# A fused attention and mixture-of-experts kernel on one core: the last attention batch interleaved with the first weights batch, and a reordered passage to the experts

## The reference, cut to what matters

```python
def attn(x, w_qkv, w_out, b_out, norm_g, norm_b):          # x: (8, 512, 256), 16 heads of 16
    q, k, v = split_heads(einsum('bnm,om->bno', x, w_qkv))
    dots = einsum('bhid,bhjd->bhij', q, k)
    norm = sqrt(sum(dots * dots, axis=-1, keepdims=True))
    attn = dots / maximum(norm, 1e-12) * norm_g + norm_b
    return einsum('bnm,om->bno', merge(einsum('bhij,bhjd->bhid', attn, v)), w_out) + b_out

def ffn(x, norm_gamma, slot_norm_gamma, slot_embeds, w1, b1, w2, b2):
    xn, sn = rmsnorm(x, norm_gamma), rmsnorm(slot_embeds, slot_norm_gamma)
    logits = einsum('bnd,esd->bnes', xn, sn)               # 8 experts, 128 slots each
    dispatch = softmax(logits, axis=1)                     # over the tokens
    combine = softmax(logits.reshape(b, n, e * s), axis=-1)
    slots = einsum('bnd,bnes->besd', xn, dispatch)
    h = gelu(einsum('besd,edh->besh', slots, w1) + b1)     # hidden 1024
    eo = einsum('besh,ehd->besd', h, w2) + b2
    return einsum('bmd,bnm->bnd', eo.reshape(b, e * s, 256), combine)

x = x + layernorm(attn(layernorm(x), ...))
x = x + layernorm(ffn(layernorm(x), ...))
```

## Time and profile before

| | |
|---|---|
| median of 3 runs | 873.18 us (872.75 to 873.45) |
| profiled execution | 873.14 us |
| its span in the profile | 870.5 us |
| mean granted clock of TensorE | 0.989 |
| attention, to the last back | 0 to 159 us |
| the last back and weights batch 0 | 159 to 203 us |
| weights batches 1 to 7 | 203 to 396 us |
| passage to the experts | 396 to 416 us |
| experts | 416 to 773 us |
| combine | 773 to 870 us |

### The profile page before, as it was taken

The page is one execution under the profiler, slowest core; times in us unless marked ns, Lnnn a source line. Parts: engine busy times, 40 slices in busy tenths (PEclk is TensorE's granted clock), DMA queues, the critical chain, the costliest instruction groups (busy, mean ns, idle before and its releaser), DMA issues. The chain is left out here.

```text
span 870.5 us, 16018 instructions
## 1 busy us (share of the span) xinstructions
PE 841.5 (97%) x5368; PEld 752.0 (86%) x5368; DVE 619.1 (71%) x1192; ACT 538.7 (62%) x1061; POOL 94.2 (11%) x105
## 2 busy tenths in 40 slices
PE   6999999779999999997999999999999999999998
PEld 6998999667788888885899999999999999999997
DVE  7788887658999898998665556555656564267786
ACT  5556555458776667776655555554556464467775
POOL 1200000022373323433000000000000000000000
PEclk9999999889999999998999999999999999999999
DMA  7111121041222222222302020202020205026983
GB/s 219 38 49 49 48 72 49 25 139 68 87 97 97 96 96 96 93 78 102 117 23 75 3 95 1 96 0 96 0 96 0 96 0 194 1 62 227 286 269 123
DMA packets 52283, 75.32 MB, mean 87 GB/s; under 512 B 3088, under 2 KB 33424, under 8 KB 52112
## 3 DMA queue, kind: packets, MB, share of 16 engines
q1 hardware_dynamic: 52240, 74.76, 25.4%
HBM read 49.59 MB, written 25.17 MB: 86 GB/s over the span
## 5 line engine op out<-in xcount | busy, mean ns | idle before, releaser
L883 PEld LDWEIGHTS bank<-w_r,act_r 128*128 128x128 f32 x1536 | 200.8, 191 | 11.0 <-DVE act_r L1765 0.7
L883 PE MATMUL bank<-w_r,act_r 128*128 128x256 f32 x1536 | 204.0, 283 | 0.2 <-DVE act_r L1765 0.2
L866 PE MATMUL bank<-sl_r,w_r 128*128 128x512 f32 x768 | 200.6, 397 | 3.6 <-DVE sl_r L1745 3.6
L1765 DVE TENSOR_TENSOR act_r<-act,act_r 128x512 fp32r<-128x512 f32 x128 | 88.6, 692 | 151.0 <-ACT act_r L1263 151.0
L1258 ACT ACTIVATE act<-bank,b_sb 128x512 f32<-128x512 f32 x128 | 88.0, 687 | 153.0 <-PE bank L866 153.0
L866 PEld LDWEIGHTS bank<-sl_r,w_r 128*128 128x128 f32 x768 | 138.0, 192 | 27.1 <-issue 3.9
L791 PE MATMUL bank<-disp_r,y_r 128*128 128x512 f32 x384 | 103.4, 406 | 1.0 <-DVE disp_r L1678 0.9
L766 PE MATMUL bank<-yT_r,snT 128*128 128x512 f32 x384 | 100.1, 397 | 0.0
L919 PE MATMUL bank<-eo_r,comb_r 128*128 128x258 f32 x768 | 92.5, 282 | 0.5 <-DVE eo_r L386 0.5
L919 PEld LDWEIGHTS bank<-eo_r,comb_r 128*128 128x128 f32 x768 | 92.2, 189 | 0.7 <-issue 0.7
L766 PEld LDWEIGHTS bank<-yT_r,snT 128*128 128x128 f32 x384 | 72.6, 190 | 15.7
(11 more groups left out here) (170 smaller groups left out, 1152.1 us busy)
## 6 DMA issues: line engine op xcount, KB each, us to landing
stage<-in_w SPq DMA_DIRECT2D x16, 1024.0 KB, 6.8
combine_scratch<-comb SPq DMA_DIRECT2D x64, 256.0 KB, 2.0
stage<-combine_scratch SPq DMA_DIRECT2D x4, 2048.0 KB, 9.3
snT<-combine_scratch SPq DMA_DIRECT2D x4, 2048.0 KB, 10.1
x_scratch<-stage SPq DMA_DIRECT2D x8, 512.0 KB, 3.0
x<-x_scratch SPq DMA_DIRECT2D x8, 512.0 KB, 4.0
x_d<-x_scratch SPq DMA_DIRECT2D x8, 512.0 KB, 9.7
slots_eo<-in_x SPq DMA_DIRECT2D x7, 512.0 KB, 4.3
```

The costliest lines, as they stand in the source:

```text
L866: last = pe.matmul(bank[i % RING][:, :], w1_r[q][:, a, k, j * P:(j + 1) * P], sl_r[f][:, c, k, :], start=(n == 0), stop=(n == len(steps) - 1))
L883: last = pe.matmul(bank[4 + 2 * f + c // 2][:, (c % 2) * D:(c % 2 + 1) * D], act_r[:, i % RING, a, c * S:(c + 1) * S], w2_r[q][:, w, j, :] ...
L1765: v.tensor_tensor(act_r[:, i % RING, 1, :], act[:, i % 2, :], act_r[:, i % RING, 0, :].bitcast(F32), ALU.subtract).then_inc(h_split, 1)
```

## The change

The memory of the attention stage is laid out anew, so that batch 0 of the weights stage has tiles of its own (`neg_lt0` and `disp0` in unused halves of `slots_eo`, `neg_max0`, `z_disp0`, `rz_disp0`), and `run_min` is shared by both stages. The split slots of the experts, `sl_r`, lie in `snT`.

PE's, ACT's and DVE's last attention back and first weights batch become one list each, `last_back_and_first_weights`. y of batch 0 is made in `attention(B - 1, before_y=True)`. The roots of x2 (`root_x2`, `scale_y`) are taken for batches 0 to 3, 4 to 6 and 7 apart. The end of batch 7's attention (`square_proj`, `root_proj`, `add_proj`, `square_x2`) is cut into slices in weights batches 2, 3 and 4, its last root comes in batch 5; the sums and the centring of w2's rows are placed in batches 5 to 7. SP stores x2 of batch 7 and loads the first weights after batch 3's reloads. The loops of ACT and DVE over the weights batches are written out.

In the passage, ACT's and DVE's steps have a new order, both halves of w2's subtraction go from POOL to DVE, the second slots' split goes into the first expert, whose `expert_out` is three tiles behind, and the load of the second combine batch waits for the last hidden tile.

The diff in its core: memory and helpers first, then SP, POOL, PE, ACT and DVE.

```diff
+        run_min = sb("run_min", [P, N])
+        neg_max0 = sb("neg_max0", [P, E])
+        z_disp0 = sb("z_disp0", [P, E])
+        rz_disp0 = sb("rz_disp0", [P, E])
...
-            woutT = of_stage(KD, D)
+            xn = sb("xn", [P, NT, D])
+            xn_r = sb("xn_r", [P, 2, NT, D], F32R)
+            xnT_r = sb("xnT_r", [P, 2, KD, N], F32R)
+            gram_r = sb("gram_r", [P, 2, KD, D], F32R)
...
+            sl_r = [snT[:, f].rearrange("p k (a n) -> p (k a) n", n=HALF).rearrange("p (a k) n -> p a k n", a=2)
+                    for f in range(HALVES)]
...
+        OUT_ROW_AT = [(B - 3, 3), (B - 3, 5), (B - 2, 1), (B - 2, 3), (B - 2, 5), (B - 1, 1), (B - 1, 3), (B - 1, 5)]
...
+        def last_front_finished(eng):
+
+            eng.wait_ge(heads_in_psum, B)
+            eng.wait_ge(xn_split, B)
+
+        def is_batch(b, n):
+            return isinstance(b, int) and b == n
+
+        def neg_logits(b, m):
+            return neg_lt0[:, m // 2, m % 2, :] if is_batch(b, 0) else neg_lt[:, m, :]
+
+        def dispatch(b, m):
+            return disp0[:, m % RING // 2, m % 2, :] if is_batch(b, 0) else disp[:, m % RING, :]
+
+        def dispatch_cols(b, m):
+            return [(neg_max0 if is_batch(b, 0) else neg_max)[:, m:m + 1],
+                    (z_disp0 if is_batch(b, 0) else z_disp)[:, m:m + 1],
+                    (rz_disp0 if is_batch(b, 0) else rz_disp)[:, m:m + 1]]
...
-            with sp.Fori(B - 4, B) as b:
+            for b in (B - 4, B - 3):
                 store_x2(b)
+            sp.wait_ge(y_ready, 1)
+            load_x2(1)
+            store_x2(B - 2)
             attention_finished(sp)
-            sp.wait_ge(x2_squared, B * NT)
-            sp.wait_ge(x2_stored, 16 * B)
+            sp.wait_ge(x2_stored, 16 * (B - 1))
...
                     store_combine(b - 1, m)
+
+            with sp.Fori(1, BH) as b:
+                reload_and_store(b)
+            store_x2(B - 1)
+            reload_and_store(BH)
+            sp.wait_ge(x2_squared, B * NT)
+            sp.wait_ge(x2_stored, 16 * B)
+            load_weights(0)
...
-            for u in range(2):
-                load_combine(u, u)
+            load_combine(0, 0)
+            sp.wait_ge(h_in_psum, E * HALVES * KH)
+            load_combine(1, 1)
...
-                    if centre:
-                        centre_out_rows(m)
+                    if centre and (b, m) in OUT_ROW_AT:
+                        centre_out_rows(OUT_ROW_AT.index((b, m)))
...
-            for c in range(2):
-                raw, hi, lo = weight_half(0, 1, c)
-                pool.wait_ge(w_hi[1], c + 1)
-                nc.gpsimd.tensor_tensor(lo, raw, hi.bitcast(F32), ALU.subtract).then_inc(w_split[1], 1)
+            for b in range(B - 3, B):
+                weights_of(b, centre=True)
...
+                if before_y:
+                    transpose_y(0, 0, first=True, to=0)
                 if back:
                     projection(b - 1)
-                if first_y:
-                    for m in range(2):
-                        logits(0, m, first=True)
...
+                if m == 0 or m == 1 and not last:
                     transpose_dispatch(b, E - 2 + m, first)
...
+                    if last:
+                        transpose_dispatch(b, E - 1)
...
-            def weights_of(b, u, first=False, second=False, last=False):
...
+                logits(0, 0, True)
+                outputs(b, False)
+                logits(0, 1, True)
+                norms(b)
+                logits(0, 2, True)
+                logits(0, 3, True)
+                transpose_o(b)
+                logits(0, 4, True)
+                transpose_dispatch(0, 0, True)
+                projection(b)
+                logits(0, 5, True)
+                transpose_dispatch(0, 1, True)
+                logits(0, 6, True)
+                transpose_dispatch(0, 2, True)
+                logits(0, 7, True)
+                transpose_dispatch(0, 3, True)
+                transpose_y(1, 1, True)
+                transpose_dispatch(0, 4, True)
+                fill_slots(0, 0, 0, 0, True)
+                transpose_dispatch(0, 5, True)
+                fill_slots(0, 0, 0, 1, True)
+
+            def weights_of(b, u, second=False, last=False):
 
 
                 for m in range(E):
-                    if m >= 2 or not first:
-                        logits(b, m, first)
+                    logits(b, m, False)
...
+            attention(B - 1, before_y=True)
+            last_back_and_first_weights()
             attention_finished(pe)
-            weights_of(0, 0, first=True)
...
-                    if i >= 2:
+                    if first:
+                        if i >= 3:
+                            expert_out(e, q, i - 3, first)
+                        if i == HALVES * KH - 1:
+                            expert_out(e, q, i - 2, first)
+                    elif i >= 2:
                         expert_out(e, q, i - 2, first)
                     elif not first:
...
+                if before_y:
+                    root_x2(0, B // 2)
...
+            def last_back_and_first_weights():
+
+                b = B - 1
+                square_proj(b - 1)
+                root_proj(b - 1)
+                square_x2(b - 1, 0, 3)
+                root_norm(b)
+                square_x2(b - 1, 3, 4)
+                root_x2(B // 2, B - 1)
+                exp_dispatch(0, 0, True)
+                exp_dispatch(0, 1, True)
+                round_oT(b, False)
+                for m in range(2, E):
+                    exp_dispatch(0, m, True)
+                    if m >= 3:
+                        round_dispatch(0, m - 3, True)
+                    if m == 5:
+                        round_y(0, 0, True)
+                    if m == 6:
+                        round_yT(1, first=True)
+                        round_y(0, 1, True)
+                round_dispatch(0, E - 3, True)
...
+                    if is_batch(b, 2) and m % 2:
+                        square_proj(B - 1, begin=m // 2, end=m // 2 + 1)
+                    if is_batch(b, 4) and m < NT:
+                        square_x2(B - 1, m, m + 1)
+                    if is_batch(b, b) and (b, m) in OUT_ROW_AT:
+                        sum_out_rows(OUT_ROW_AT.index((b, m)))
...
+                    if is_batch(b, 3) and m == 0:
+                        root_proj(B - 1)
+                    if is_batch(b, 5) and m == 0:
+                        root_x2(B - 1, B)
+                    exp_dispatch(b, m, False)
...
-            weights_of(0, first=True)
-            root_x2(B - 2, B)
...
+            last_back_and_first_weights()
             weights_of(1, second=True)
-            with sc.Fori(2, B - 1) as b:
+            for b in range(2, B - 1):
                 weights_of(b)
...
+            sc.wait_ge(logits_in_psum, B * E)
+            sc.wait_ge(y_split, B * KD)
+            round_dispatch(B - 1, E - 2, False)
+            keep_slots(B - 1, 0, 0)
+            round_weights(0, 0, 0, 0)
+            round_dispatch(B - 1, E - 1, False)
+            round_weights(0, 0, 0, 1)
+            exp_combine(B - 1, 0)
+            keep_slots(B - 1, 0, 1)
+            exp_combine(B - 1, 1)
+            exp_combine(B - 1, 2)
+            sc.wait_ge(slots_in_psum, (B - 1) * HALVES * KD + KD)
+            round_weights(0, 0, 1, 0)
+            exp_combine(B - 1, 3)
+            round_weights(0, 0, 1, 1)
+            keep_slots(B - 1, 1, 0)
+            for m in range(4, E):
                 exp_combine(B - 1, m)
 
...
+                    if first and i == 0:
+                        keep_slots(B - 1, 1, 1)
...
+                if before_y:
+                    scale_y(0, 0, B // 2)
...
+                if before_y:
+                    make_y(0, False)
...
+                if before_y:
+                    for k in range(KD):
+                        rest_of_yT(0, k, at=0)
...
+
+                b = B - 1
+                keep_proj(b - 1, False)
+                times_q(b)
+                keep_logits(0, 0, True)
+                add_proj(b - 1)
+                keep_logits(0, 1, True)
+                clamp_norm(b)
+                scale_o(b)
+                keep_logits(0, 2, True)
+                invert_sum(0, 0)
+                keep_logits(0, 3, True)
+                invert_sum(0, 1)
+                rest_of_oT(b)
+                keep_logits(0, 4, True)
+                invert_sum(0, 2)
+                fold_min(0, 1, True)
+                rest_of_dispatch(0, 0)
+                invert_sum(0, 3)
+                keep_logits(0, 5, True)
+                keep_proj(b, False)
+                rest_of_dispatch(0, 1)
+                invert_sum(0, 4)
+                make_y(1, False)
+                keep_logits(0, 6, True)
+                rest_of_dispatch(0, 2)
+                invert_sum(0, 5)
+                keep_logits(0, 7, True)
+                fold_min(0, 2, True)
+                rest_of_dispatch(0, 3)
```

(48 more changed lines are left out.)

273 lines of the change are left out of this document (121 added, 152 removed).

## The result

The changed kernel takes **857.63 us** (median of 4 runs, 857.30 to 857.68) against 872.96 (872.08 to 873.45) of the kernel before in the same series: a ratio of 0.9822, 95% interval 0.9811 to 0.9834. That is 15.3 us less; 14.7 were forecast. The profiled execution took 857.62 with a span of 855.7, 14.8 under the 870.5 of before.

What follows compares the result with a forecast made beforehand. PE was taken as the bound, busy 841.5 of 870.5 us, with idle holes and half clock to recover. Interleave -10.1, weights batches +0.6, passage -5.2 sum to -14.7 from 873.14: 858.4 us, range 854.0 to 865.0.

Steps and rivals of the forecast that it cites:

- The five waits foretold: Interleave: PE still waits before projection(7), batch 1's y transpose, dispatch tile 4's transpose, first fill, transposed minimum; 4.5 us together.
- The clock's term: Last attention back and first weights batch: matmuls granted 1.2 GHz lose 4.0 us of PE busy time.
- the 0.8 let through to PE for the slices: Batch 3: four slices add 1.85 us to DVE; 0.43 fits idle time, 0.8 of the other 1.4 reaches PE.
- the first of the two values: Passage: gain 6.1 us at 2.4 GHz, against 4.8 if idle time before hidden tile 0 brings 1.2 GHz.
- The 2.2 us "lost" at half clock: Passage: the experts' first 18 matmuls take 6.82 us, not about 4.65, behind 3.55 us idle; 2.2 us lost.
- Rival A: Interleave and passage: holes close only partly and the clock falls in them; 2 us each, 862.4 us; chance 0.19.
- Rival B: Interleave's end: bound by DVE's put-off folds before the minimum; 8 of 10.1 us go, 866.4 us; chance 0.07.
- C: Batches 3 and 5: ACT's table switch costs twice its load, some 2.0 us each reach PE; 862.4 us; chance 0.03.
- D: Weights batches: straight code instead of ACT's and DVE's loops slows instruction supply; +23 us, 881.4 us; chance 0.04.
- E: Interleave and passage: the change does nothing, another unseen wait ends both stretches; 873.1 us; chance 0.02.
- The covers named at nothing: SP's later load_weights(0) and load_combine(1) cost nothing; the weights load 1 to 2 us if late.

Runs made afterwards that it cites:

- the two experiments: Kernel before with only the passage's edits: 867.86 us, ratio 0.9944; changed kernel with the passage's edits reversed: 863.16 us, ratio 0.9887.
- the undone passage: Changed kernel with the passage to the experts put back as it was, slots' halves staying in snT: 863.16 us, ratio 0.9887.
- three of the edited kernels: Changed kernel with the passage put back (hole 2.70): 863.16 us; with w1 and slots ahead of combine shifts (3.12): 860.28 us; the third is not identified.
- a fourth: Changed kernel with POOL's normalisation ahead of y's low half in batch 0: 860.44 us, ratio 0.9848.
- a fifth: Changed kernel with w2's two subtractions of the first expert on POOL again: 859.77 us, ratio 0.9855.
- batch 4's experiment: Changed kernel with add_proj's four additions moved from batch 3 to tiles 0 to 3 of batch 4, squares two tiles later: 857.17 us, ratio 0.9819.

## Why the prediction was right

The total was right (858.4 against 857.63), and the mechanisms of both parts were, but that the total is this close is partly luck: three terms were off by 1.5, 1.9 and 0.8 us, with different signs.

- **Interleave, 10.1 forecast, 11.57 measured.** The causes stand as foretold. The five waits foretold were 1.1, 0.3, 1.0, 0.7 and 1.4; measured 1.07, none, 0.72, 0.64 and 1.43, with the releasers named. One sign did not come: the largest wait is the one before the minimum, not the projection's (the prediction's own list has it so). The start of gram_times_q was to be 160.3 and is 160.03, but it moves by more than that from kernel to kernel. Idle time gave 6.77, forecast 6.1. The clock's term was 4.0 us of busy time; PE's busy time in the stretch fell by 5.53, of which some 0.7 (an estimate from eight transposes at 0.09 us) is the transposes of y moved ahead. That leaves 4.8; no run says whether the 0.8 above the forecast is the clock's.
- **Weights batches, 0.6 forecast, 2.49 measured.** Batch 2 gave its gain (0.46 of 0.6). The step that failed is the 0.8 let through to PE for the slices. It took the slices at their own length (four in 1.67 us in the kernel before, 0.42 each) and missed that POOL's subtraction runs in two of the places, though the same contention was used, with its rows, for the passage. One slice measured 1.61, a minimum 1.77. By the prediction's own test, a weights batch of over 28 us, this step was wrong: batch 3 took 29.62. All losses of the batches together are 2.95 us, just within the stated end of 3.0. The other sign, no wait of PE over 1 us, held: the longest is 0.83.
- **Passage, 5.2 forecast, 6.01 measured** over the marks, 4.8 and 5.5 by the two experiments. The first hidden tile came 3.41 us nearer (3.5 foretold). The clock did not fall, so the first of the two values, 6.1, less the 0.3 given back, was the right one (5.8); the middle was taken for want of a reason. The 2.2 us "lost" at half clock in the kernel before cost nothing there, as the undone passage shows; the sum did not use them.
- **Rival A** did not occur. Its mechanism is real, though: half clock followed a hole of 2.7 to 3.1 us in three of the edited kernels and three holes of 1.3 to 1.9 us within 11 us in a fourth, and in a fifth, with a hole of 3.03, three runs had a lower mean clock. In the change no hole from gram_times_q to the end is over 1.43.
- **Rival B** is out: the last wait is 1.43. **C** is out in the form given: an exponential followed its load by 1.30 us, and in its cover the switch costs 0.05 us of ACT and nothing on PE that shows. Moved by two tiles it costs 2. **D** is out: the straight batches 1, 5 and 6 take 27.35, 27.51 and 27.34 us, as the loop's did. **E** is out.
- The covers named at nothing held: SP's later weights load and load_combine(1) show no wait. load_combine(1) is issued at 754.08 and ACT's first use is at 765.70, 11.6 us later ("10 us or more" foretold); such a load takes 9.2 to land. The weights load holds by little, if the reading of batch 4's experiment is right: 3 us later in the batch, a combine store behind it cost 2 us.
- **The range.** Its lower end, 854.0, goes below what its terms give (12 + 6.3 - 0.6 us of gain, 855.4) by an unnamed 1.4 us. Nothing hung on it.

Open: the passage alone in the kernel before is worth 0.9 us less than in the changed kernel (381.54 against 380.66 from T7 to load), half of it before the first hidden tile, half behind; no run tells why. Whether DVE's lead over POOL decides who is held, as the four cases look, would want a run that moves only that.

## What to carry to other kernels

When work is put into the idle time of VectorE, look at what GpSimd does in that very place, and which of the two comes first; a one-column operation can cost 1.3 us there, and a whole slice one tile away 0.6. A wait that looks useless may be what keeps two engines apart, so an edit that removes it is priced by what then runs side by side. A tighter order that shortens one matmul gap and lengthens the next can lose: here 1.42 us went, 3.12 came, and half clock stood behind them. Matmuls at half clock cost nothing where the next one would wait anyway.

## What the runs showed of the hardware

- A VectorE operation with two operands in SBUF waits for GpSimd's operation to end, whatever its own size: 1 column 1.34 us, 256 columns 1.61, both ending within 0.3 us behind GpSimd's. The other way round GpSimd waits: its subtraction takes 1.72 us instead of 1.30. A minimum of VectorE that begins 0.36 us before GpSimd's normalisation ends takes 0.90 instead of 0.68.
- Beside GpSimd, VectorE's tensor_scalar from SBUF to SBUF, with one tensor operand, doubled too (four in 2.78 us against 1.36). An operation with one operand in PSUM stayed at 0.68.
- Two holes of PE of 1.46 and 1.49 us, 6 us apart, left the granted clock at 1.00; three of 1.28, 1.35 and 1.90 us within 11 us were followed by 0.76. Holes of 2.70 and 3.12 us were followed by 1.2 GHz for part of the next 8 us (mean 0.79). A hole of 3.55 us was followed by 1.2 GHz in the kernel before and by full clock in the kernel with the passage undone. At 1.2 GHz six hidden matmuls took 1.2 us more.
